# A two-layer graph-attention and mixture-of-experts kernel: TensorE signals twice an expert tile in place of four times, and SyncE's looped loads are written out

## What is computed

```python
x = x + gnn(layernorm(x), adj, a0..a3)      # attention within each graph, four edge kinds
x = x + ffn(layernorm(x), gate_w, gate_b, w1, w2, w3)

def ffn(x, ...):                            # 16384 tokens, 16 experts, hidden 256
    probs = softmax(x @ gate_w + gate_b)
    top_probs, top_idx = top_k(probs, 2); top_probs /= sum(top_probs)
    hidden = silu(x @ w1[e]) * (x @ w2[e])
    return sum over the two experts e of top_probs[e] * (hidden @ w3[e])
```

## Time and profile before

| | |
|---|---|
| median of 3 runs | 867.44 us (866.37 to 876.1) |
| the profiled execution | 875.39 us, of which the span of the instructions is 873.6 us |
| mean granted TensorE clock over the span | 0.937 |
| busy share: TensorE matmuls, VectorE, ScalarE, GpSimd | 85%, 58%, 48%, 59% |

### The profile page before, as it was taken

The page is one execution under the profiler, slowest core; times in us unless marked ns, Lnnn a source line. Parts: engine busy times, 40 slices in busy tenths (PEclk is TensorE's granted clock), DMA queues, the critical chain, the costliest instruction groups (busy, mean ns, idle before and its releaser), DMA issues.

```text
span 873.6 us, 17532 instructions
## 1 busy us (share of the span) xinstructions
PE 739.4 (85%) x4422; PEld 595.1 (68%) x4423; DVE 503.5 (58%) x1706; ACT 415.4 (48%) x1011; POOL 516.7 (59%) x670
## 2 busy tenths in 40 slices
PE   3899999999999766888988888987898888878895
PEld 2465656565666645677878777886787777777785
DVE  3799999999999863545454544543333233233332
ACT  7999999999999221222222222222222222222221
POOL 3337777778787765554645455554555645545555
PEclk9999999999999767999989988998999999999998
DMA  5233544332321144766666555634766565666640
GB/s 157 73 109 115 157 129 147 96 105 81 105 90 35 33 148 156 216 220 190 225 213 197 171 184 168 197 126 131 232 212 190 178 211 179 197 200 198 189 131 8
DMA packets 127462, 133.28 MB, mean 153 GB/s; under 512 B 16362, under 2 KB 98545, under 8 KB 127378
## 3 DMA queue, kind: packets, MB, share of 16 engines
q1 hardware_dynamic: 107008, 94.66, 36.0%
q0 software_dynamic: 15616, 34.38, 11.6%
q10 hardware_dynamic: 4754, 3.25, 1.2%
HBM read 52.28 MB, written 41.19 MB: 107 GB/s over the span
## 4 chain that ended last, share of the span: by engine, by line
PE 43%; DVE 23%; issue 16%; another core or an unknown queue 12%; ACT 4%; POOL 1%; DMA 0%; DVEq 0%; ACTq 0%; POOLq 0%
PE psS L1258 23%; PE bank L1283 13%; DVE stage L886 3%; PE bank L1273 3%; DVE stats L817 3%; DVE late L933 3%; DVE bestix L909 2%; DVE late L949 2%; DVE X L1083 1%; PE psS L1166 1%; ACT silu L736 1%; DVE late L968 1%; DVE best L905 1%; ACT late L689 1%
## 5 line engine op out<-in xcount | busy, mean ns | idle before, releaser
L1258 PE MATMUL psS<-X,late 128*128 128x256 f32 (+1 forms) x1280 | 264.1, 355 | 6.0 <-issue 5.8
L1258 PEld LDWEIGHTS psS<-X,late 128*128 128x128 f32 x1280 | 212.7, 203 | 26.0 <-issue 7.1
L1083 DVE TENSOR_TENSOR X<-silu,psS 128x512 f32<-128x512 f32 x144 | 98.8, 686 | 226.2 <-remote 119.8
L736 ACT ACTIVATE silu<-psS 128x512 f32<-128x512 f32 x144 | 86.0, 597 | 282.3 <-remote 147.2
L632 POOL DMA_INDIRECT second_list<-xin x144 | 142.2, 988 | 129.7 <-DVE xin L1092 88.7
L643 POOL DMA_INDIRECT out_dram<-xin x144 | 141.7, 984 | 122.4 <-DVE xin L1092 82.7
L1283 PE MATMUL bank<-wts,X 128*128 (+1 forms) x1152 | 168.1, 292 | 36.5 <-DVE X L1083 33.5
L1283 PEld LDWEIGHTS bank<-wts,X 128*128 128x128 f32 x1152 | 150.6, 203 | 45.9 <-issue 45.8
L583 POOL DMA_INDIRECT first_list<-stage,slot x128 | 128.1, 1001 | 52.6 <-issue 41.2
L1092 DVE SCALAR_TENSOR_TENSOR xin<-bank,xin 128x128 f32<-128x128 f32 x288 | 87.5, 346 | 100.7 <-remote 62.3
L1166 PE MATMUL psS<-late,hT 128*128 128x512 f32 x256 | 118.7, 607 | 3.0 <-ACT late L689 2.8
(11 more groups left out here) (156 smaller groups left out, 826.0 us busy)
## 6 DMA issues: line engine op xcount, KB each, us to landing
late<-wts SPq DMA_DIRECT2D x160, 256.0 KB
xin<-second_list SPq DMA_DIRECT2D x48, 262.0 KB
X<-in_x_dram SPq DMA_DIRECT2D x32, 256.0 KB
late<-in_adj_dram SPq DMA_DIRECT2D x32, 256.0 KB
xin<-first_list SPq DMA_DIRECT2D x48, 134.0 KB
xin<-second_list SPq DMA_DIRECT2D x48, 131.0 KB
wts<-in_L_ffn_w_dram SPq DMA_DIRECT2D x48, 128.0 KB
xin<-first_list SPq DMA_DIRECT2D x48, 67.0 KB
```

The lines of the kernel that those rows point to most:

```text
L736: nc.scalar.activation(silu[:, u % 2, :], psG[u % 2], ACT.Silu).then_inc(s_silu[u % TURNS], 1)
L1083: v.tensor_tensor(hid[:, u % HIDS, :], silu[:, u % 2, :], psU[u % 2], ALU.mult).then_inc(s_hid[u % TURNS], 1)
L1258: last = mm(out[:, c * W2 + rows.start:c * W2 + rows.stop], at[:, half * H + c * P:half * H + (c + 1) * P], xT[:, u % XTS, rows], start=Tr ...
```

## The change

Four edits that belong together, and one on SyncE:

- `s_G` is gone. TensorE signals once, `s_U`, after both halves. `silu` waits for that.
- `s_xTp` is one semaphore, and is signalled only where no w3 product follows the transposes (`if not experts`): three times at the start of each round, for tiles 0, 1 and 2.
- Elsewhere the copy to `xT` waits for `s_Y` of the w3 product that TensorE runs right after those transposes (`turned`).
- `load_whole_turns` on SyncE has no loop any more: 24 loads a round with constant wait values and constant places in the list, and without `s_turn`.

```diff
-        s_xTp = [sem(f"s_xTp{i}") for i in range(TURNS)]
+        s_xTp = sem("s_xTp")
...
-        s_G = [sem(f"s_G{i}") for i in range(TURNS)]
...
             def load_whole_turns(r, word_of):
-                with sp.Fori(r * TURNS_EACH + 1, r * TURNS_EACH + EARLY_TURNS) as n:
-                    for u in range(S):
-                        sp.wait_ge(s_z[u], n * 32)
-                        sp.sem_inc(s_turn, 1)
-                        load_whole(r, word_of(r, (n - r * TURNS_EACH) * S + u), u)
+                for i in range(S, EARLY_TURNS * S):
+                    sp.wait_ge(s_z[i % S], (r * TURNS_EACH + i // S) * 32)
+                    load_whole(r, word_of(r, i), i % S)
...
+            def turned(n, u, i, d):
+
+
+                if i is None or i > 0:
+                    done(act, s_Y, n, u, -LAG)
+                else:
+                    k = n * S + u + d
+                    act.wait_ge(s_xTp, k // TILES * (LEAD + 1) + k % TILES + 1)
+
             def tile(n, u, i, on):
                 if on(0):
                     done(act, s_hid, n, u, -2)
-                    done(act, s_G, n, u, 0)
+                    done(act, s_U, n, u, 0)
                     nc.scalar.activation(silu[:, u % 2, :], psG[u % 2], ACT.Silu).then_inc(s_silu[u % TURNS], 1)
                 for d in offsets(i, turned_after):
                     k = (u + d) % S
                     done(act, s_U, n, u, d - XTS)
-                    done(act, s_xTp, n, u, d)
+                    turned(n, u, i, d)
...
-                    for half, out, s_out, s_free in ((0, psG[u % 2], s_G, s_silu), (1, psU[u % 2], s_U, s_hid)):
+                    for half, out, s_free in ((0, psG[u % 2], s_silu), (1, psU[u % 2], s_hid)):
...
-                        last.then_inc(s_out[u % TURNS], 1)
+                    last.then_inc(s_U[u % TURNS], 1)
...
-                    last.then_inc(s_xTp[k % TURNS], 1)
+                    if not experts:
+                        last.then_inc(s_xTp, 1)
```

## The result

The changed kernel takes 876.73 us in the median (867.85 to 888.3, 20 runs), the kernel before on the same chip 870.12 (866.37 to 876.1, 20 runs). The ratio is 1.005, with a 95% interval of 1.003 to 1.0071. So the change costs about 4 us by that ratio (6.6 by the two medians), where 12 to be gained were forecast: within 2%, inside the range, and of the wrong sign. The ratio leaves out three slow executions of after, and the profiled one (881.12 us, span 879.4) is among them, so a difference of a few microseconds between the two profiles is not to be read.

What follows compares the result with a forecast made beforehand. TensorE was taken as the bound, losing 110 us in the expert stage. Terms -15 - 5 + 8 + 0 = -12 us on the profiled 875.4 give 863.4, ratio 0.986, so 855 from the 867.4 median; range 826 to 877.

Steps and rivals of the forecast that it cites:

- What bounds the kernel: Expert stage: TensorE is busiest, and 110 us are lost there, mainly to stops and the lower clock level.
- Signals get through one at a time, 3 us apart: TensorE's held signals: pass singly about 3 us apart during GpSimd's scatter runs, until all piled up come at once.
- The count of holds: Both rounds: 33 stops taken as long holds (runs of six scatters), 28 as short ones (runs of four).
- Long holds, -15 us: Runs of six scatters: up half's signal passes first, `hid` earlier; 8 x 1.4 + 8 x 0.5 = 15 us gained.
- Short holds, +8 us: Runs of four scatters: copy waiting for w3 makes new 0.5 us stops, 7 us, plus 1 us for the up half.
- The clock, -5 us: TensorE's lower clock level: one in five of the 27 us at stake comes back, 5 us; bounds 0 and 13.
- Increments, 0: TensorE: 576 signals become 294; an increment costs nothing that can be seen, so 0 us.
- SyncE, 0: SyncE's written-out loads: transfers are hidden by some 20 us of lead, so cost 0.
- The slack: Tile without a hold: 1.6 us left for `silu` and 2.4 us for the copy, so both moved waits cost 0.
- The end of the hold decides everything: Rival, chance 0.23: TensorE resumes when GpSimd's run ends; gain and loss cancel, 866 us, -2 to +8.
- The slack given up: Slower rival, chance 0.14: hold of the up signal costs 1.3 us for 0.6; 28 x 0.7 = 20 us, 887 at most.

Runs made afterwards that it cites:

- whole_again: The whole change once more against the kernel before, on a chip with held signals: 869.1 us for 864.11, ratio 1.0052.
- silu_on_up_b: Kernel before with the halves signalling once and `silu` waiting for the up half, where signals are held: 874.35 us for 863.16, ratio 1.016.
- its one-line form: Kernel before with only `silu`'s wait moved to the up half, gate half still signalling, where signals are held: 871.46 us for 863.76, ratio 1.0133.
- ten_signals: Kernel before plus six more TensorE increments a tile on a semaphore nobody reads, where signals are held: 862.88 us for 864.11, ratio 0.9996.
- pe_only: Change without its `load_whole_turns` edit against the kernel before, where nothing is held: 740.92 us for 740.41, ratio 1.001.
- pe_only_b: Both TensorE parts without SyncE's against the kernel before, another run where nothing is held: 742.15 us for 740.08, ratio 1.0029.
- sp_only: Only SyncE's loads written out against the kernel before, where nothing is held: 740.22 us for 740.41, ratio 0.9992.

## Why the prediction was wrong

**What bounds the kernel** was right. 110 us are lost in the expert stage to holds and the clock; without them it takes 182 and 201 us a round, 108 us less than in the earlier trace rows.

**Signals get through one at a time, 3 us apart** was the wrong reading. The rows were right, but the clock of it is GpSimd's and not the signal's own. From the trace's semaphore increments: in most runs of four scatters what is pending gets through 5.7 to 6.3 us after the run's first scatter. In a run of six the end is at +8.6 to +9.2, and most have earlier passes, anywhere from +2.8 to +8.1. Who gets one of these goes by when it asked, that is, by the end of the last record of its matmuls. In the trace of before, of the held signals of runs of six that asked at +2.0 to +3.5, 18 of 19 passed before the end; of those from +4.0 on, all but one came at the end. In the earlier trace rows the gate half asked at +3.2 and passed at +6.0; the up half, asking at +4.1, came at the end. I had put the 3 us between them to the account of the signals.

**The count of holds** was off too. 33 long and 28 short ones were assumed. Counted as runs of scatters that start less than 1.6 us apart, the trace of before has 21 of six and 34 of four, that of after 11 of six and 41 of four. So GpSimd's runs are not given from outside, as the prediction took them to be: they changed with the change. What this is worth was not measured.

**Long holds, -15 us,** is the step that failed. It said of the up half that it "passes 3 us later at the latest", and so that `hid` is 1.4 us earlier. The up half asks about 0.9 us later than the gate half did, at +3.8 to +4.7, and with that comes at the end in 10 of the 11 runs of six of after. Nothing stands ahead of it: where the trace has the w3 signal before it, that had passed before the up half asked. In the profile of after 19 up signals were held for more than 3 us, 16 in `whole_again` and 19 in `silu_on_up_b`, and `hid` started 0.7 to 1.0 us after the signal had passed, 0.81 in most. Before, 17 of 26 such signals had `hid` there less than 0.1 us after, because `silu` was done; behind the other nine it took 0.7 to 1.0 us too. 19 holds, of which two thirds now lose 0.7 us, are an estimated 9 us lost, 13 if all do; `silu`'s part alone measured 11.2 us (874.35 less 863.16) and its one-line form 7.7. The price was of the right size, its sign wrong. The rows that I had also speak for it: `hid` in the earlier trace rows starts right at the end of the hold, with `silu` out of the way.

**Short holds, +8 us.** Right in size: idle time before the halves went from 6.0 to 15.3 us, +9. In kind it is shown in part: the view of waits puts 3.0 us, eight stops of at most 0.5, down to the copy to `xT`; the rest are shorter gaps and stops without a named releaser. That the copy's part then costs only 0.2% alone was not foreseen. There its stops replace others before the transposes.

**The clock, -5 us,** had the wrong sign in all. Round 0 rose from 0.92 to 0.95, as said, but round 1 fell from 0.97 to 0.92. By the prediction's own working that loses 33 us in place of 27. `whole_again` has 0.94 and 0.93 where `ten_signals`, on the same chip, has 0.94 and 0.96: 32 us in place of 24. So as much as the whole loss can lie in the clock of round 1; no run separates it from the later `hid`.

**Increments, 0,** was right, as `ten_signals` shows, and so is **SyncE, 0**, where nothing is held. **The slack** of 1.6 and 2.4 us was right as well: without holds both moved waits cost 0.1% (`pe_only`) to 0.3% (`pe_only_b`), with few 0.14%.

**The rivals.** "The end of the hold decides everything" (866 us) had the mechanism nearly right, but called gain and loss equal. "The slack given up" named the loss of 0.7 us a hold, and its price, 28 x 0.7 = 20 us, was too high because it put it on the short holds. The measured +4 us lies between the two. The profile of before could have told more by one more step: reading where in GpSimd's run each signal asked and passed, for all 21 runs of six in place of two. The up half comes at the end in 16 of them.

## What to carry to other kernels

A merged signal delays its first reader to the end of the whole group. That is free while signals come at once, and when they are held it puts that reader's own work (here 0.6 us of `silu`) behind the hold. So read for a delayed signal what sets the time of its arrival, counted from the start of each candidate on the other engines, before its removal is priced. Here the remedy lay on GpSimd (3% by spacing its scatters, on a chip that holds), and not on the engine that stopped.

## What was not expected of the hardware

- The same kernel takes 740 us on two chips and 863 to 873 on two others. On the first none of TensorE's signals was held, even in a run of 88 scatters each 1.3 to 1.4 us after the one before (`sp_only`, round 0). DMA packets take about the same on both (175 and 182 ns in the median for 4192 bytes). One of the chips that hold did so in all three sets of runs on it (864, 863 and 873 us); the other chips were each seen in one set. Why one holds signals and the other does not was not found.
- On a chip that holds, it depends on how GpSimd issues its scatters: with pairs 2.8 to 3.0 us apart 159 of 243 signals of round 1 were held, with pairs 3.39 us apart and a wait between them 21 of 176, with one scatter a tile none of 232.
- In a run of six scatters, signals that asked 2.0 to 3.5 us after its first scatter mostly passed before the end (18 of 19), those that asked after 4.0 us did not (all but one).
- Six and more added semaphore increments a tile on TensorE, 960 in all, cost nothing: 0.9996 (0.9965 to 1.0026).
